# Expert rows kept as fp16 pairs and transposed by the load, in a gated two-layer block with a routed mixture of experts

## What is computed

```python
x = x + tanh(g_ffn[1]) * _L1_ffn_ref(_layernorm(x), router_w, w_in, b_in, w_out, b_out)

logits = x2 @ router_w;  probs = softmax(logits);  top_p, top_e = top_k(probs, 2)
for e in range(8):                                # on the rows that chose expert e
    h = gelu(xd @ w_in[e] + b_in[e])              # 256 -> 256
    y = h @ w_out[e] + b_out[e]                   # 256 -> 256
out[token] += y * p
```

## Time and profile before

| | us |
|---|---|
| median of 3 runs | 473.06 |
| lowest, highest | 472.47, 476.5 |
| the profiled execution | 474.49 |
| its span | 472.6 |
| last expert scatter issued (start) | 461.11 |
| granted TensorE clock, mean | 0.969 |

### The profile page before, as it was taken

The page is one execution under the profiler, slowest core; times in us unless marked ns, Lnnn a source line. Parts: engine busy times, 40 slices in busy tenths (PEclk is TensorE's granted clock), DMA queues, the critical chain, the costliest instruction groups (busy, mean ns, idle before and its releaser), DMA issues.

```text
span 472.6 us, 13099 instructions
## 1 busy us (share of the span) xinstructions
PE 394.9 (84%) x4092; PEld 308.3 (65%) x4092; DVE 368.8 (78%) x1416; ACT 331.4 (70%) x671; POOL 268.7 (57%) x313
## 2 busy tenths in 40 slices
PE   2758899998999989999899987789559999979850
PEld 1536667776776777677686765568438897967740
DVE  2888888998988889899789786367655667779994
ACT  2855788898889889898879877566706666646640
POOL 2522112545454364626545565769988888888870
PEclk9998999999999999999999999899959999999996
DMA  7245576664565555875553774624335569396985
GB/s 242 83 139 163 180 214 179 196 181 141 177 213 170 166 171 167 221 204 184 180 174 111 223 220 121 198 68 130 101 126 143 170 175 332 116 341 251 323 275 204
DMA packets 69500, 87.10 MB, mean 184 GB/s; under 512 B 9485, under 2 KB 55290, under 8 KB 69306
## 3 DMA queue, kind: packets, MB, share of 16 engines
q1 hardware_dynamic: 60074, 65.81, 46.7%
q0 software_dynamic: 6816, 18.65, 10.8%
q10 hardware_dynamic: 2544, 1.81, 1.2%
HBM read 51.07 MB, written 35.18 MB: 182 GB/s over the span
## 4 chain that ended last, share of the span: by engine, by line
PE 42%; POOL 17%; issue 14%; DVE 10%; DMA 8%; ACT 6%; ACTq 0%; POOLq 0%; DVEq 0%; SPq 0%
PE ps_J L1650 12%; PE ps_F L1650 6%; POOL store_y L771 6%; DMA store_y<-y_out,y_row 6%; PE ps_O L1764 5%; PE ps_T L1659 5%; POOL store_x L765 5%; PE ps_S L1751 5%; POOL pause_t L778 5%; PE ps_R L1689 2%; PE ps_O L1775 2%; PE ps_G L1650 2%; DMA temp_t<-in_temp 1%; DVE y_out L2934 1%; DVE xb_lo L2903 1%
## 5 line engine op out<-in xcount | busy, mean ns | idle before, releaser
L771 POOL DMA_INDIRECT store_y<-y_out,y_row x78 | 81.4, 1044 | 21.8 <-issue 16.5
L765 POOL DMA_INDIRECT store_x<-xn_E,slot_u x64 | 68.0, 1063 | 26.5 <-DVE slot_u L2633 13.6
L1089 ACT ACTIVATE prob<-ps_S 128x512 f32<-128x512 f32 x128 | 72.4, 594 | 12.7 <-PE ps_S L1751 10.0
L778 POOL TENSOR_TENSOR pause_t<-half_ones,minus_half 128x2 f32<-128x2 f32 x71 | 54.7, 770 | 1.9
L1751 PE MATMUL ps_S<-q_stack,k_stack 128*128 128x256 f16 x256 | 44.5, 276 | 5.9 <-issue 3.8
L2922 DVE TENSOR_TENSOR h_lo<-h_f,h_hi 128x512 f16<-128x512 f32 x39 | 26.9, 689 | 21.0 <-ACT h_hi L1173 9.4
L1650 PE MATMUL ps_J<-wout_hi,h_hi 128*128 x112 | 31.2, 278 | 14.3 <-DVE y_out L2934 10.9
L1764 PE MATMUL ps_O<-prob,v_wide 128*32 128x128 f32 x1024 | 41.0, 279 | 1.1 <-ACT prob L1089 0.5
L1165 ACT ACTIVATE h_f<-ps_F,bin_t 128x256 f32<-128x256 f32 x56 | 23.4, 470 | 24.5 <-PE ps_F L1650 18.9
L751 POOL TENSOR_TENSOR rstd_C<-var_C,minus_half 128x2 f32<-128x2 f32 x16 | 12.1, 759 | 40.4 <-DVE var_C L2412 40.4
L1650 PE MATMUL ps_F<-xb_hi,win_hi 128*128 128x256 f16 x112 | 31.7, 283 | 3.9 <-DVE xb_lo L2903 3.3
(11 more groups left out here) (301 smaller groups left out, 1399.5 us busy)
## 6 DMA issues: line engine op xcount, KB each, us to landing
parts_scratch<-parts SPq DMA_DIRECT2D x32, 256.0 KB
k_stack<-parts_scratch SPq DMA_DIRECT2D x64, 128.0 KB
q_stack<-parts_scratch SPq DMA_DIRECT2D x128, 64.0 KB
xb<-store_x SPq DMA_DIRECT2D x30, 257.0 KB
y_got<-store_y SPq DMA_DIRECT2D x14, 512.0 KB
c_in<-in_ctx SPq DMA_DIRECT2D x16, 256.0 KB
x_in<-in_x SPq DMA_DIRECT2D x16, 256.0 KB
store_x<-zeros SPq DMA_DIRECT2D x15, 257.0 KB, 4.6
```

Of the source, the lines that this page charges most:

```text
L765: pool.indirect_dma_start(store_x, bass.IndirectOffsetOnAxis(slot_u[q][:, at:at + 1], 0), xn_e[q][:, at, :], None).then_inc(s_scat[q], 16)
L771: pool.indirect_dma_start(store_y, bass.IndirectOffsetOnAxis(y_row[n][:, b:b + 1], 0), y_out[n][:, b, :], None).then_inc(s_y_kept[n], 16)
L778: pool.tensor_tensor(pause_t[:, :], half_ones[:, :], minus_half[:, 0:2], ALU.pow).then_inc(s_set_p, 1)
L1089: act.activation(prob[m % PROBS][:, 2 * n:2 * n + 2, :, :], bank_s[n], ACT.Sigmoid, scale=float(HD) ** -0.5).then_inc(s_prob[n], 1)
```

## The change

1. **Rows as fp16 parts.** `rows_hi` on ScalarE takes the place of `normed_e`: the same two ACTIVATE a pair, with an fp16 result into the first 512 bytes of each row. `normed_e` moves to VectorE: two `tensor_scalar` of 128x256 a pair that write the normed rows once in fp32 (`xn_f`), which the router's transposes read and from which the low part is made. `rows_lo` on GpSimd, one `tensor_tensor` of 128x1024 a pair, subtracts and writes the low fp16 parts into the next 512 bytes. A scatter now waits for `rows_lo` of its pair, and moves as many bytes as before.
2. **Transposing loads.** `load_block` issues two DMAs: 256 rows of 512 fp16 values with `transpose=True` into `xb` as [128, 4, 256], high parts then low parts, and 8 bytes of every row, which hold the row number, into `row_no`. `transpose_block`, `copy_hi` and `copy_lo` are gone; `layer1` reads `xb` directly and waits for the load. A ring buffer is free when `layer1` and `take_rows` of its last tile are done.
3. **Three bank sets.** The hidden and the result banks are three each (`HB = 3`, `side(i) = i % 3`), and so are `h_f32`, `h_hi`, `h_lo`. The first layer runs two tiles ahead of the second instead of one.
4. **Fewer pauses.** The pause between the halves of tiles 0 to 35 is gone (36 of 71). Those between scatters of rows stay, and so do the ones after tiles 0, 1 and 2.
5. The loops over the tiles are written out; their order is otherwise the one above. The banks for the last sums move (`copy_x3`).

```diff
-XB, YB, CHUNK = 5, 5, 8
+XB, YB, CHUNK, HB = 5, 5, 8, 3
+        e_hi, e_lo = ([t[:, :, 0:D].bitcast(F16)[:, :, c:c + D].rearrange("p (b k) d -> p b k d", b=2) for t in xn_e]
+                      for c in (0, D))
+        xn_f = w_f32[:, KT - 1, WCOLS - 2 * D:WCOLS].rearrange("p (b d) -> p b d", b=2)
-        hid_banks = [... for n in ("F", "S0")]
-        y_banks = [... for n in ("J", "S1")]
+        hid_banks = [... for n in ("F", "S0", "R")]
+        y_banks = [... for n in ("J", "S1", "O")]
         def side(i):
-            return 0 if i <= EARLY else (i - EARLY) % 2
+            return i % HB
@@ load_block
                 for j in [j for j in range(i) if home(j) == n][-1:]:
-                    sp.wait_ge(s_xb_t, j + 1)
+                    sp.wait_ge(s_h, j + 1)
                     sp.wait_ge(s_y_row, j + 1)
-                sp.dma_start(xb[n][:, :, :], store_x[bass.ds(row_at(i, 0), BLK), :]
-                             .rearrange("(p b) c -> p b c", b=SUB))
+                sp.dma_start(xb[n][:, :, :], store_x16[bass.ds(at, BLK), 0:2 * D], transpose=True).then_inc(done, 16)
+                sp.dma_start(row_no[n][:, :, :], store_x[bass.ds(at, BLK), D - 1:WIDE].rearrange("(b p) c -> p b c", b=SUB))
@@ gpsimd
+            def rows_lo(p):
+                pool.wait_ge(s_rows_hi, 2 * p + 2)
+                pool.wait_ge(s_xn["E"], 2 * p + 2)
+                pool.tensor_tensor(e_lo[p % 2], xn_f[:, :, :].unsqueeze(2).broadcast_to([128, 2, TOP, D]), e_hi[p % 2],
+                                   ALU.subtract).then_inc(s_rows_lo, 1)
             def scatter(p, at):
+                pool.wait_ge(s_rows_lo, p + 1)
...
             keep_block(0, 0)
-            long_pause()
             keep_block(0, 1)
             long_pause()
...
             keep_block(2, 1)
             long_pause()
+            rows_lo(15)
             scatter(15, 3)
...
-            for i in range(4, TILES):
-                keep_block(i, 0)
-                if i < CLOSE:
-                    long_pause()
-                keep_block(i, 1)
+            keep_block(4, 0)
+            keep_block(4, 1)
...
@@ scalar
-            def normed_e(p):
-                normed("E", p, lambda b: xs[...].broadcast_to([128, TOP, D]), lambda b: xn_e[p % 2][...])
+            def rows_hi(p):
+                    act.activation(e_hi[q][:, b, :, :], xs[:, 2 * p + b:2 * p + b + 1, :].broadcast_to([128, TOP, D]),
+                                   ACT.Identity, bias=shift["E"][q][:, b:b + 1], scale=rstd["E"][q][:, b:b + 1])
-            def copy_hi(i):
-                act.activation(xb_hi[q][:, :, :], xb_banks[side(i)], ACT.Copy).then_inc(s_xb_hi, 1)
@@ tensor
-            def transpose_block(i):
             def layer1(i, m):
-                    pe.wait_ge(s_xb_lo, i + 1)
+                    loaded(pe, i)
-                               [(xb_hi[q][:, k, :], xb_lo[q][:, k, :]) for k in range(KT)])
+                               [(tile[:, k, :], tile[:, KT + k, :]) for k in range(KT)])
...
             layer1(1, 0)
             layer1(1, 1)
+            layer1(2, 0)
+            layer1(2, 1)
             layer2(0, 0)
             layer2(0, 1)
-            transpose_block(3)
...
@@ vector
+            def normed_e(p):
+                need(dve, s_t["E"], p)
+                need(dve, s_rows_lo, p)
+                for b in range(2):
+                    dve.tensor_scalar(xn_f[:, b, :], xs[:, 2 * p + b, :], mv["E"][q][:, b, 0:1], rstd["E"][q][:, b:b + 1],
+                                      ALU.subtract, ALU.mult).then_inc(s_xn["E"], 1)
-            def copy_lo(i):
-                dve.tensor_tensor(xb_lo[q][:, :, :], xb_banks[side(i)], xb_hi[q][:, :, :], ALU.subtract)
             shifts("E", 0)
+            normed_e(0)
```

More of the change, by code:

```diff
@@ L413, in build, with last_at @@
         block = st.enter_context(nc.Block())
+        store_x16 = store_x.bitcast(F16)
         def side(i):
-            return 0 if i <= EARLY else (i - EARLY) % 2
+            return i % HB
+        def last_at(k):
+            return max(i for i in range(TILES) if side(i) == k)
         def home(i):
@@ L774, in _, with pause @@
             paused = itertools.count(2)
+            def pause():
+                pool.wait_ge(s_set_p, next(paused))
+                pool.tensor_tensor(pause_t[:, :], minus_half[:, 0:2], minus_half[:, 0:2], ALU.add).then_inc(s_set_p, 1)
             def long_pause():
@@ new lines, in _ @@
+            add_bias(15)
+            take_rows(18)
+            hidden_lo(17)
+            add_bias(16)
+            take_rows(19)
+            hidden_lo(18)
+            add_bias(17)
+            take_rows(20)
+            hidden_lo(19)
+            add_bias(18)
+            next(gates)
+            take_rows(21)
+            hidden_lo(20)
+            add_bias(19)
+            next(gates)
+            take_rows(22)
+            hidden_lo(21)
+            add_bias(20)
+            next(gates)
@@ new lines, in _ @@
+            take_rows(23)
+            hidden_lo(22)
+            add_bias(21)
+            next(gates)
+            take_rows(24)
+            hidden_lo(23)
+            add_bias(22)
+            next(gates)
+            take_rows(25)
+            hidden_lo(24)
+            add_bias(23)
+            next(gates)
+            take_rows(26)
+            hidden_lo(25)
+            add_bias(24)
+            next(gates)
+            take_rows(27)
+            hidden_lo(26)
+            add_bias(25)
@@ new lines, in _ @@
+            next(gates)
+            take_rows(28)
+            hidden_lo(27)
+            add_bias(26)
+            add_pair(0)
+            take_rows(29)
+            hidden_lo(28)
+            add_bias(27)
+            add_pair(1)
+            take_rows(30)
+            hidden_lo(29)
+            add_bias(28)
+            add_pair(2)
+            take_rows(31)
+            hidden_lo(30)
+            add_bias(29)
+            add_pair(3)
+            take_rows(32)
+            hidden_lo(31)
+            add_bias(30)
```

657 lines of the change are left out of this document (502 added, 155 removed).

## The result

The changed kernel took 496.69 us (median of 4 runs, 493.92 to 497.78), the kernel before 473.15 beside it: ratio 1.0474, 95% interval 1.0407 to 1.0541. Timed once more on another chip it gave 496.08 us and 1.0484 (1.0405 to 1.0564). It is 23.5 us slower where 12 us faster was forecast. The profiled execution has a span of 496.0 us.

The account below looks back on a forecast made before the run. In the tiles GpSimd was taken as nearly full (3.40 us a tile), TensorE close behind (3.06). Span: 472.6 - 20.5 + 0 + 3.7 + 1.5 + 3 = 460.3, with 0.5 more 461 us; range 446 to 492 (8 in 10).

Parts of the forecast that it names:

- the 3 for the DMA engines: Crowded last 60 us: they get shorter while their bytes stay, costing +3 us, between 0 and 6.
- `rows_lo` at nothing: First stage, GpSimd: 15 `rows_lo` of 2.0 us fit into 31.0 us of idle time, so cost nothing.
- one sign of being wrong: The prediction is wrong if the first stage grows by over 8 us or the tile pace stays at 3.1 or more.
- the second rival: The first stage takes back what the tiles give: 473 us, no change; chance 0.10.
- `normed_e` at +3.7: First stage, VectorE: two new instructions a pair, 11.2 us in all, a third on the path: +3.7, between 0 and 13.2.
- Before tile 3 at 0: Before tile 3: three pauses go (-1.9), `rows_lo(15)` comes in (2.0); together 0, between -1 and +1.
- Tiles 3 to 26 at 2.77 a tile: Tile stage: TensorE without transposes paces at 2.62 plus 0.15 lost, 2.77 us for each of 24 tiles.
- the third rival: Scatters without a pause take longer, GpSimd needs 3.25 us a tile: -5 instead of -20.5, 476 us; chance 0.08.
- SyncE's queue at +1.5: First two block loads, now two DMAs each, stand ahead of the last pair's steps on SyncE: +1.5 us, at worst +4.
- The transposing loads at 1.6 us a block: DMA engines: 1.3 us for 1024 pieces plus 0.3 for row numbers; with the scatter 2.3 a tile, under 2.77.
- The first rival: Transposing loads pace the tiles on the 16 DMA engines: 475, about 490, or 520 or more; chance 0.24.
- The last eleven tiles at 2.9: Last 11 tiles, where VectorE also adds pairs: 3.4 less 0.68 is 2.7; taken as 2.9 us a tile.

Follow-up runs that it names:

- e1: Changed kernel with `rows_lo` cut to 2 of 1024 elements, low parts zeroed once at the start (part of the computation left out): 476.73 us.
- e2: Changed kernel with each `rows_lo` replaced by two GpSimd memsets of the same 1024 elements a partition and a tiny one: 485.02 us.
- e13: Changed kernel with `rows_lo` cut to 128x2, low parts zeroed, and five results' loads one by one between block loads: 471.37 us, ratio 0.9941.
- e5: Changed kernel with `transpose_e(15)`, `logits(15)` and `ranks(15)` put back behind the layers on TensorE: 506.0 us, on a chip with slow tiles.
- e12: Changed kernel with `rows_lo` on VectorE, pair 15's router steps back behind the layers, five results' loads between block loads: 471.08 us, ratio 0.9954.
- e6: The kernel before, with only the 36 pauses between a tile's two scatters taken out: 464.7 us, ratio 0.9821.
- e11: Changed kernel with the pause put back between the two scatters of each of tiles 0 to 35: 510.03 us, ratio 1.0732.
- e14: Changed kernel with the five first results' loads one by one between the block loads on SyncE: 490.2 us, ratio 1.0342.
- e8: Changed kernel with each transposing load replaced by a plain load of the same 256 KB, so tiles compute on other numbers: 506.68 us.

## Why the prediction was wrong, step by step

The sum was 460.3 us of span, the profile has 496.0. By the same four points (36.2 is 11 x 2.9, the 3 for the DMA engines and 1.3 for the last half tile):

| stretch | forecast, us | measured | error |
|---|---|---|---|
| first block load | 287.4 + 3.7 | 309.1 | +18.0 |
| from it to tile 3's store | 53.5 + 1.5 | 61.9 | +6.9 |
| tile 3 to tile 27 | 24 x 2.77 = 66.5 | 77.5 | +11.0 |
| tile 27 to the last store | 36.2 | 35.3 | -0.8 |
| the rest | 11.5 | 12.2 | +0.7 |

**`rows_lo` at nothing: the step that failed most, +21.6 us (e1).** Its duration was right (2.07 us for 2.0), though by luck: the 0.74 was taken for the start of an instruction, and e1's subtraction of 128x2 takes 0.21 in all. Its cover was not right. I took GpSimd's idle time, 31.0 us in total before `rstd_E`, as room for 30 us of work, and asked only what waits for GpSimd. Two things failed. GpSimd's occupation alone cost 10 us (e2); that idle time lies in front of `rstd_E`, which the next pair's norm waits for, but how the 10 divide between that wait and held-up VectorE instructions is not shown. And with its reading, an instruction of VectorE that met `rows_lo` stood until it was through, with TensorE's idle time and lower clock behind it (the other 11). I had named the price of a missing cover, "up to 2 us each", and not taken the case into any rival; at 1.4 us a pair it was close to that. So one sign of being wrong, a first stage longer by over 8 us, is there; the second rival had the right stage by other terms (`normed_e` and SyncE), and stopped at 473.

**`normed_e` at +3.7.** It cost 0.15 in e1 and 2.5 in e13, within the spread. VectorE took in its 11.8 us nearly free; the 19.4 us of `rows_lo`, moved there too, cost 5 to 9.

**Before tile 3 at 0.** The pauses went as costed. But `transpose_e(15)`, `logits(15)` and `ranks(15)` moved forward past two layers on TensorE, and I did not look at a step moved on the engine that the layers share: 4.6 us of waiting and what hangs on it, 7.3 us in e5, back to 53.5 us in e12. Part of what hangs on it is TensorE's clock: from tile 0's store to tile 3's it is granted 0.90 in the changed kernel, 1.00 in the kernel before and in e12.

**Tiles 3 to 26 at 2.77 a tile: right.** 2.66, by TensorE's two halves of 1.31 (busy 39.03 of 40 us from 380 to 420). Scatters without a pause took 0.96 us, so the third rival fell. That GpSimd's pauses held the old pace is shown from both sides, by e6 and e11.

**SyncE's queue at +1.5: the right queue, the wrong place.** I asked what two transposing loads delay at the front of the queue. At 2.05 us a block where 0.70 stood, 39 of them are 80 us of SyncE, where tiles 3 to 27 take 77.5; the results' loads stand behind all of them, and I had left them out (the +3 for the DMA engines was about bytes). The stall of 14 us ahead of tile 27 is its price, partly paid back: e14 gains 6 to 7 us where it is removed.

**The transposing loads at 1.6 us a block: somewhat low.** The page has 60653 packets under 512 B where it had 9485, 1312 more a block: the 1024 pieces and 256 row numbers of the forecast, nearly. From 380 to 420 us q1's 76.3% of 16 engines are 488 us for 20458 packets: 24 ns each, not 20, and 1.9 us a block (16 blocks of 1280 packets): neither the 1.1 of today's load nor the 10.5 of eight squares one after another. With the scatters' 0.7 that is 2.6 us a tile, as much as TensorE needs. The first rival, pieces pacing the tiles, did not happen, but only just: TensorE was busy 39.03 of 40 us at a DMA share of 1.05. That the time came out near this rival's 490 is chance.

**The last eleven tiles at 2.9.** 3.1 here ((35.34 - 1.27) / 11), inside the forecast with its +3, and only while the stretch before is late; once it is not, 3.5 (e12, in the same way).

## What to carry to other kernels

Idle time of an engine is cover only if it lies where the new work will stand, and if the work does not hold up a neighbour: look at the longest, not only the mean, of the *other* engine's unchanged instructions before and after. When a kind of DMA changes, multiply its issue time by its count and ask what stands at the end of that queue. And try the cheapest part of a change alone: here, taking 36 pauses out of the old kernel gave 1.8%, and the whole change, repaired, gave 0.5%.

## What the hardware showed that I had not expected

- A GpSimd instruction of 2.07 us (128x1024, two operands read) can hold an instruction of VectorE, else 0.2 to 0.7 us long, until it ends: beside ten of sixteen stood one of 1.5 to 3.1 us. Beside memsets of 0.96 us the longest `var_E` took 1.46 us, and `picks` stayed at 209 ns on the mean.
- A transposing load of 256x512 fp16 holds SyncE's issue for 1.23 us, with its companion 2.05 us a block; a plain load of the same bytes in e8 0.55, with its companion 1.39.
- Such a load, with its companion, took 1.9 us of all 16 DMA engines; a plain one in e8 1.1 (35.7% of 40 us for 6623 packets, some 13 blocks).
- Versions of the changed kernel without pauses ran their tiles at 2.6 to 2.7 us on three chips or more and at 3.3 to 3.4 on another, where the kernel before was only 0.6% slower.
